# The tail of a one-core layer kernel: who adds two partial sums, and in which order two quads' rows are turned

## The reference

```python
logits = x @ router_w.T                       # x: layernorm of h, 448 x 512
rw, sel = top_k(softmax(logits), 8);  rw = rw / sum(rw)
for e, wg, wu, wd in experts:
    w_e = sum(where(sel == e, rw, 0))
    acc = acc + (silu(x @ wg) * (x @ wu)) @ wd * w_e[:, None]
return h + acc
```

## Time and profile before

| | us |
|---|---|
| median of 3 runs | 351.6 (351.4 to 351.88) |
| the profiled execution's own time | 349.6 |
| its span | 347.8 |
| TensorE busy | 298.8 (86%) |
| VectorE busy | 148.8 (43%) |
| ScalarE busy | 127.6 (37%) |
| GpSimd busy | 147.0 (42%) |

### The profile page before, as it was taken

How to read it: one execution, slowest core, us unless ns; L and a number is a source line. 1 busy time by engine, 2 the same in 40 slices (tenths; PEclk the granted TensorE clock), 3 DMA queues, 4 the chain that set the end, 5 groups by cost and what they waited for, 6 DMA issues and landing times.

```text
span 347.8 us, 3769 instructions
## 1 busy us (share of the span) xinstructions
PE 298.8 (86%) x1133; PEld 158.3 (46%) x1133; DVE 148.8 (43%) x446; ACT 127.6 (37%) x208; POOL 147.0 (42%) x138
## 2 busy tenths in 40 slices
PE   6799794284886999989999999999999999997880
PEld 1344341142553644545545555555555555553230
DVE  3437769726578681314352423323233232422430
ACT  3236716995587340212231322223222232322100
POOL 5404434664445203243535354453544535344260
PEclk9999987558998967999999999999999999999997
DMA  7999902547504936999999999999999999956832
GB/s 296 374 388 419 372 15 98 176 136 248 161 1 148 325 114 201 264 298 299 315 329 285 286 292 323 314 331 338 313 290 301 317 306 324 270 102 88 208 92 78
DMA packets 23556, 85.50 MB, mean 246 GB/s; under 512 B 3585, under 2 KB 3713, under 8 KB 22769
## 3 DMA queue, kind: packets, MB, share of 16 engines
q1 hardware_dynamic: 15152, 64.54, 54.6%
q0 software_dynamic: 7984, 20.26, 25.0%
q10 hardware_dynamic: 402, 0.48, 0.4%
HBM read 72.34 MB, written 12.92 MB: 245 GB/s over the span
## 4 chain that ended last, share of the span: by engine, by line
PE 69%; DVE 11%; issue 6%; ACT 6%; DMA 4%; POOL 1%; ACTq 0%; DVEq 0%
PE ps L1051 22%; PE ps L1080 15%; PE ps L878 9%; PE ps L1071 4%; DMA scrap<-token_rows,idx 3%; PE ps L1035 2%; PE ps L1100 2%; PE ps L1110 2%; PE ps L928 2%; PE ps L1131 2%; PE ps L954 2%; ACT w_t L696 2%; PE ps L1062 2%; DVE raw L1293 1%; DVE amax L1340 1%
## 5 line engine op out<-in xcount | busy, mean ns | idle before, releaser
L595 POOL DMA_INDIRECT scrap<-token_rows,idx x36 | 35.9, 997 | 98.4 <-DVE idx L1435 80.1
L606 POOL DMA_INDIRECT sum<-w_t,add_idx x32 | 50.8, 1588 | 15.2 <-issue 8.4
L1447 DVE SCALAR_TENSOR_TENSOR w_t<-ps,scrap,w_t 128x192 f32<-128x192 f32 x32 | 13.4, 418 | 100.1 <-issue 89.2
L812 ACT ACTIVATE w_t<-ps 128x192 f32<-128x192 f32 x34 | 11.3, 331 | 90.5 <-PE ps L1051 87.6
L523 POOL TENSOR_TENSOR root_out<-root_in,minus_half 112x1 f32<-112x1 f32 x20 | 12.8, 640 | 60.1 <-DVE root_in L1205 59.9
L878 PE MATMUL ps<-raw,last 128*112 128x512 f32 x64 | 32.4, 659 | 4.3 <-issue 2.3
L1051 PE MATMUL ps<-ring,w_t 128*128 128x384 f32 x96 | 34.2, 499 | 0.4 <-ACT w_t L807 0.4
L928 PE MATMUL ps<-w_t,scrap 128*112 128x512 bf16 (+1 forms) x96 | 27.2, 444 | 8.1 <-DVE h L1243 4.6
L818 ACT ACTIVATE w_t<-ps 128x512 f32<-128x512 f32 x32 | 19.1, 597 | 37.2 <-PE ps L1080 37.2
L1051 PE MATMUL ps<-big,w_t 128*128 128x384 f32 x88 | 31.3, 499 | 0.0
L807 ACT ACTIVATE w_t<-ps 128x512 f32<-128x512 f32 x34 | 20.3, 597 | 18.7 <-PE ps L1071 14.5
(11 more groups left out here) (188 smaller groups left out, 464.5 us busy)
## 6 DMA issues: line engine op xcount, KB each, us to landing
big<-in_ffn_gate_up SPq DMA_DIRECT2D x15, 768.0 KB, 7.6
ring<-in_ffn_gate_up SPq DMA_DIRECT2D x13, 768.0 KB, 7.3
big<-in_ffn_w_down SPq DMA_DIRECT2D x15, 384.0 KB, 5.7
ring<-in_ffn_w_down SPq DMA_DIRECT2D x13, 384.0 KB, 5.6
raw<-in_ffn_gate_up SPq DMA_DIRECT2D x6, 768.0 KB, 6.7
last<-in_ffn_gate_up SPq DMA_DIRECT2D x6, 768.0 KB, 8.2
big<-in_mlp_w_in SPq DMA_DIRECT2D x2, 1536.0 KB, 16.6
big<-in_mlp_w_in SPq DMA_DIRECT2D x2, 1280.0 KB, 19.7
```

What stands on the lines that cost most here:

```text
L595: nc.gpsimd.indirect_dma_start(got[:, s, :], None, rows_dram[:, :], bass.IndirectOffsetOnAxis(ap=idx[:, s:s + 1], axis=0)).then_inc(ld_got ...
L606: nc.gpsimd.indirect_dma_start(acc_dram[m.two][:, :], bass.IndirectOffsetOnAxis(ap=add_idx[:, m.four:m.four + 1], axis=0), y[:, m.four, :] ...
```

## The change

1. VectorE adds the two sums instead of GpSimd, inside the quad loop, after `find` and before the four adds of L1535. It waits for all three loads. GpSimd goes from its loads straight to the gathers of the next pair, then waits for VectorE's four adds and clears `part[1]` (so that a second turn of the loop would add zeros).
2. The copy of the last tile's y out of PSUM moves from ScalarE to VectorE, ahead of the tables of the quad loop, with a semaphore of its own, `y_last`.
3. TensorE turns b's rows right behind a's, before gate/up a.
4. VectorE's order becomes: weigh a, turn_back a, weigh b, find a', turn_back b, find b' (before: weigh a, weigh b, turn_back a, find a', turn_back b, find b').

```diff
             def scatter(m):
-                pool.wait_ge(y_ready, m.upto())
+                if m.t == NE - 1:
+                    pool.wait_ge(y_last, 1)
+                else:
+                    pool.wait_ge(y_ready, m.upto())
...
-            pool.wait_ge(ld_part[0], 16)
-            for g in range(NG):
-                if g % 2 == 0:
-                    pool.wait_ge(ld_part[1 + g // 2], 16)
-                nc.gpsimd.tensor_tensor(part[0][:, g, :], part[0][:, g, :], part[1][:, g, :], ALU.add).then_inc(total_ready, 1)
+            pool.sem_inc(cleared, 1)
             for k, n_pairs in pairs_of(pool, pairs_i, table_ready):
                 for i in range(2):
                     gather(Quad(k + 1, i))
+                pool.wait_ge(total_ready, 4 * k + 4)
+                pool.sem_inc(scatter_go, 1)
+                nc.gpsimd.memset(part[1][:, :, :], 0.0).then_inc(cleared, 1)
...
-            y_out(Tile(NE - 1))
...
                 transpose_x(a)
+                transpose_x(b)
                 gate_up_lists(a)
-                transpose_x(b)
                 gate_up_lists(b)
...
+            m = Tile(NE - 1)
+            dve.wait_ge(y_done, m.upto())
+            dve.wait_ge(added[m.two], m.added() - 32)
+            nc.vector.tensor_copy(y[:, m.four, :], bank(4 + m.two)).then_inc(y_last, 1)
...
-                    weigh(m, gate_w[:, m.i:m.i + 1])
-                for m in two:
-                    turn_back(m)
-                    find(Quad(k + 1, m.i))
-                dve.wait_ge(total_ready, NG)
+                weigh(two[0], gate_w[:, 0:1])
+                turn_back(two[0])
+                weigh(two[1], gate_w[:, 1:2])
+                find(Quad(k + 1, 0))
+                turn_back(two[1])
+                find(Quad(k + 1, 1))
+                dve.wait_ge(cleared, k + 1)
+                for n in range(3):
+                    dve.wait_ge(ld_part[n], 16)
+                for g in range(NG):
+                    nc.vector.tensor_tensor(part[0][:, g, :], part[0][:, g, :], part[1][:, g, :], ALU.add).then_inc(total_ready, 1)
+                dve.wait_ge(total_ready, 4 * k + 4)
```

More of the change, by code:

```diff
@@ L363, in program @@
         spread_done = sem("spread_done")
+        y_last = sem("y_last")
         total_ready = sem("total_ready")
+        cleared = sem("cleared")
         place_done = sem("place_done")
@@ L1084, in down_lists @@
                 pe.wait_ge(ht_ready, m.upto())
-                pe.wait_ge(y_ready, m.upto(-2))
+                pe.wait_ge(y_ready, m.upto(-2 - m.i))
+                pe.wait_ge(y_last, 1)
                 for c in range(2):
@@ L1107, in spread_lists @@
                         if g == 0:
-                            pe.wait_ge(y_ready, m.upto())
+                            pe.wait_ge(y_ready, m.upto(-1))
                             pe.wait_ge(where_ready, 2 * m.k + (m.i + 1))
```

## The result

The changed kernel takes 346.09 us (median of 4 runs, 345.52 to 347.11), the kernel before 351.74 (4 runs, 351.4 to 352.24): a ratio of 0.9845, 95% interval 0.9816 to 0.9875. The prediction was 348.4, range 347.2 to 350.3. So how far the time misses the forecast is uncertain. That the sum had the wrong terms does not hang on it, as the traces show.

The account below looks back on a forecast made before the run. It took the quads' chain, then the landing of group 3's store, then a fixed tail as the bound. 2.44 us from the chain plus 0.8 from the store made 3.2 off 351.6: 348.4 us, range 347.2 to 350.3.

Parts of the forecast that it names:

- A tail that I take as fixed: Behind the last store's landing no engine or DMA works until the span ends: 5.5 us, assumed unchanged.
- My last rival: The end hangs on something other than the last store, so the earlier chain gains nothing: 351.6 us, chance 0.05.
- ScalarE freed, b's rows behind a's, turn_back a first: TensorE's chain after the last tile: 0.49, 1.43 and 0.52 us earlier, down a 2.44 us earlier in all.
- The last y on VectorE: Copy after the last tile: 0.69 us on VectorE, scatter at most 0.1 us later, loop tables hidden with 1.1 us to spare.
- the rival of a scatter held by the tables: Last scatter waits for VectorE's loop tables, loads land 1.8 us late, VectorE ends 1.3 late: 349.7 us, chance 0.07.
- the reading of tile 30's scatter: It ran beside the loop's tables in 1.57 us, no longer than the last one's 1.55: evidence against a held scatter.
- The two sums on VectorE: Before the spread's adds: second load lands at 330.4, sums take 2.46 us, off the path with 0.49 us slack.
- the gathers run into the loads: First gather, issued while sums still load, goes ahead of the last load; VectorE ends 0.8 us late: 349.2, chance 0.12.
- GpSimd: memset 2.1 us: GpSimd's clearing of the second sum costs 2.1 us, from about 333.7 to 335.8, before the last store lands.
- the rival that it does: GpSimd's memset holds VectorE's adds of the spread, the last ending 1.7 us late: 350.1 us, chance 0.06.
- the slower one built on it: The memset is itself stretched by 4.4 us and holds VectorE's adds, so the kernel takes 354.4 us; chance 0.03.
- The stores: With the gathers done before them, the last store lands in 3.0 us instead of 3.8: 0.8 us gained.

Follow-up runs that it names:

- the first edit alone: The kernel before with only VectorE adding the two sums; 345.95 us, ratio 0.983. With VectorE also clearing the second sum: 345.02 us, 0.9775.
- the repeat: The changed kernel, unchanged, run again on the chip of later runs beside the kernel before: 346.93 us, ratio 0.9892.
- the loop one turn shorter: The changed kernel with VectorE clearing the second sum and GpSimd's gather loop running one turn less: 344.41 us, ratio 0.9727.
- changed kernel with VectorE clearing: The changed kernel with VectorE instead of GpSimd clearing the second sum, behind its last add: 345.9 us, ratio 0.9803.
- gathers behind loads: The changed kernel with GpSimd waiting for the three loads of the sums before issuing the two gathers: 350.54 us, ratio 0.9995.
- the same with VectorE clearing: The changed kernel with GpSimd's gathers waiting for the sums' loads and VectorE clearing the second sum: 349.91 us, ratio 0.9975.

## Why the prediction was wrong, step by step

*"A tail that I take as fixed", 5.5 us: wrong, and the cause of the miss.* The step failed at its first look: I saw that no engine and no DMA was busy behind the last store and asked no further what the end waited for. It waited for GpSimd's drain of 5.87 us, which began at 341.7 with the landing of the second gather, and which stands in the trace of the kernel before. With it my own numbers would have given another sum: GpSimd's last work is the memset, which I had ending at 335.8, and 5.87 us behind it is 341.7; the last store, at 339.0, no longer counts; the end is then at 341.9, 5.9 us earlier, and the time 351.6 - 5.9 = 345.7 us. Measured: 346.09. That this comes so near is in part luck: behind Y it puts the end at 341.9 - 315.77 = 26.1, and the two profiles have 27.6 and 27.0, since the memset waited for sums that came late (below). My last rival, that the end hangs on something other than the last store, was right in its condition and wrong in its price: it took for granted that this something would stay where it was, while the change moves it.

*ScalarE freed, b's rows behind a's, turn_back a first: right.* Forecast against measured, us behind Y: gate/up a 1.18, 1.19 (318.19); down a 7.63, 7.46 (324.46); the spread 12.39, 12.15 (329.15).

*The last y on VectorE: right.* 0.69 us, the last scatter 1.49 us behind Y against 1.40 before. VectorE's tables ran from 318.10 and the scatter from 318.49, in the 1.55 us of before, landing in 4.8 us: the rival of a scatter held by the tables falls. But the reading of tile 30's scatter, on which I had leaned, was incomplete. In the kernel before it took 1.57 us beside the tables, and the copy of `pick` beside it took VectorE 0.52 us, where the next one took 0.22. With the first edit alone, with and without VectorE clearing, the same scatter took 1.80 us and that copy 0.21. So either one engine or the other lost 0.2 to 0.3 us there. What cost these tenths at tile 30's scatter, no run here tries.

*The two sums on VectorE: price right, start wrong.* Four adds took 2.50 us, 2.46 forecast. They were to start at 330.45 + 1.23 for the later Y, and started at 334.02. The second load landed 2.3 us late, at 334.0: it took 9.62 us where I had taken 6.9, while the first gather, issued 2.35 us behind it, moved its rows in the same time (326.63 to 334.3, 7.7 us). This is the rival "the gathers run into the loads", and it was no minor one: I had priced it at 0.8 us at the last add and gave it 0.12; the last add came 2.0 us later than without gathers (22.1 against 20.1), and 1.4 in the repeat. On the repeat's chip the second load takes 7.4 us without gathers and 9.0 with them. Over all profiles it took 6.8 to 7.8 us in the seven in which no gather was issued before it landed, 8.4 and 8.6 with the gathers 4.7 us behind it (first edit alone, with and without VectorE clearing), 8.8 to 9.6 in four of the five with the gathers where the change puts them, and 7.8 in the fifth (the loop one turn shorter). So the gathers as the cause are well supported, but one profile speaks against them, and why is open. "They are behind it in GpSimd's own queue" was no protection.

*GpSimd: memset 2.1 us, measured 1.81.* It did not hold VectorE's adds: L1550 took 2.48 us for four beside it, so the rival that it does, and the slower one built on it, fall. But the memset was on the path all the same, by way of the drain.

*The stores: right.* 3.0 us to landing, as taken.

So the gain is not made by the earlier chain. It is made by GpSimd ending 4.4 us earlier, from 31.8 to 27.4 behind Y, and the chain's edits add nothing measurable to it (0.983 with the first edit alone, 0.9845 and 0.9892 with all), because the late sums and GpSimd's end hide them.

Two things stay unsettled. The runs show that GpSimd's drain sets the end, not what GpSimd does in it. And Y moves by up to 4 us from one execution to the next, with the same instructions ahead of it; between the two profiles compared here it moved by 1.2, which is why their spans differ by 3.2 us and the stretch behind Y by 4.4. The granted clock is at most a part of it: from 80 to 110 us it was 0.94 in the kernel before and in the changed one, whose Y is 1.2 us apart, and 0.83 in the repeat, whose Y is 3.0 us later still. None of these runs tried it, nor whether it is what makes the medians gain 5.65 us in one group and 3.8 in another.

## What to carry to other kernels

Before calling a tail fixed, find what each engine's queue does in it: an engine with a long end of its own (here GpSimd, whose drain took 5.87 us, against 17 ns on VectorE) has to be done early, and work on it for which nothing waits is not free there (two memsets cost 3.4 of their 3.7 us). Keep GpSimd's last work, an unused prefetch or a clearing above all, well ahead of the last store, or give it to an engine with a short end: with the memset on VectorE, VectorE's drain ended within 0.1 us of the memset (343.0 and 341.0 + 2.08 = 343.1, changed kernel with VectorE clearing). And check what else is on the DMA engines when a transfer is moved forward: order in one engine's queue did not keep a later transfer from slowing an earlier one in four profiles of five (the second load of sum 1 took 8.8 to 9.6 us in these four, against 6.8 to 7.8 where no gather was issued before it landed).

## What the runs showed of the hardware that was not expected

- GpSimd's last drain took 5871 ns in the six profiles in which its last wait was for the gathers' landing; VectorE's took 17 (2078 to 2080 where a memset of 1.76 us was its last work), ScalarE's 8, SyncE's 7.
- Begun while a memset ran, it ended 5.87 us behind the memset (338.48 to 344.35). Begun at 325.5, right behind the issue of the loads, it took 10.27 us, and these runs don't show why.
- With GpSimd's gather issued 1.9 us after VectorE's adds of two SBUF tensors had started, the gather took 1.47 us instead of 1.05 (gathers behind loads, and the same with VectorE clearing). That the adds held it was not tried by itself.
- The scatter of tile 30 took 1.80 us instead of 1.57 in two profiles (the first edit alone, with and without VectorE clearing); in the kernel before it took 1.57, and VectorE's copy of `pick` beside it 0.52 instead of 0.21.
- Four adds of 112x512 with both operands in SBUF took 2.50 us, and with one in PSUM 2.48.
- A loop counted at run time whose start equals its bound ran its body once (the version with the loop one turn shorter, whose trace holds both gathers, at 328.7 and 331.2).
